# The PV product of an attention kernel in two halves of its columns, with the score products in pairs

## The chip, the cores and the metric

The kernel runs on one core of one Trainium2 chip. Its five engines run side by side and are joined by semaphores: PE (TensorE, the matrix unit), DVE (VectorE), ACT (ScalarE), POOL (GpSimd) and SP (SyncE, which here only starts transfers). PE writes its products to PSUM, eight banks of 128 partitions x 512 fp32. The metric is the device time of one execution in microseconds. Before the change it is 2535.62 us, the median of 3 runs (2533.4 to 2536.08).

## What is computed

The input is x, 4 sequences of 1024 tokens with 128 features. Three layers follow each other: a transformer block with attention and a mixture of experts, a retention layer, and the same transformer block again. Each works on the normalised x and is added to it. The part around the change is the attention of the block, which runs twice:

```python
q = (h @ Wq).reshape(Bb, Ss, H, Dh)      # Bb = 4, Ss = 1024, H = 16 heads, Dh = 8
k = (h @ Wk).reshape(Bb, Ss, H, Dh)
v = (h @ Wv).reshape(Bb, Ss, H, Dh)
scores = jnp.einsum('bqhd,bkhd->bhqk', q, k) / jnp.sqrt(jnp.float32(Dh))
attn = jax.nn.softmax(scores, axis=-1)
ctx = jnp.einsum('bhqk,bkhd->bqhd', attn, v).reshape(Bb, Ss, Dd)
x = x + ctx @ Wo
...
wts, idx = jax.lax.top_k(probs, K)       # K = 2 of 8 experts
h1 = jax.nn.gelu(jnp.einsum('td,edf->etf', xt, W1) + b1[:, None, :])
```

## The kernel before

A layer of attention is 16 groups (`GROUPS`): each is one sequence and four heads. A group has 16 steps s. One step handles 128 keys of one half (512) of the queries for the group's four heads, and at the same time the maxima of the next group:

- `score(layer, g, s, u)`, u = 0 to 3 (L1162): the scores of head u, 128 keys x 512 queries, one product of 51 rows. Its 51 rows are 48 of a product of q and k cut into bf16 parts, and 3 that subtract the row maximum. Heads 0 and 2 lie in the lower 64 rows of the array, heads 1 and 3 in the upper. Each goes to the next bank of a ring of three (`RING`, `s_slot`): PE waits on `s_taken` until ScalarE has read what stood there three slots ago.
- `top(layer, g + 1, s, pair)`, pair = 0, 1 (L1176): the scores of two heads of the next group with the queries on the partitions, a pair of products in the lower and the upper rows, into two banks. `m_slot` waits on `max_taken` until VectorE has read what was put there two slots ago.
- `weigh` (L1189), here called PV: the exponentials of the step two back, times v. Four products, one per head, of 128 rows by 32 columns; each fills its own quarter of the partitions of one bank (`PV_BANK`), and eight steps accumulate there. The fp32 product runs as two passes, so that a trace has eight records for it. v carries a column of ones, which gives the softmax sum.
- `aside` puts single products between S1 and the first maximum pair: the transpose of the maxima ("nm", L1145) at steps 3 and 12, and in groups 0, 1, 4, 5, 8 and 9 the projection of a later chunk of x ("turn" L1103 at step 1, "k" and "q" L1132 at steps 5 and 7, "v" L1138 at step 9). They use a slot of the ring of three.
- `turn_context` (L1103) transposes what PV has summed, at steps 4 and 12, after ScalarE copied it to `ct` (L637, at steps 2 and 10). The next PV of the same bank waits for that copy (`ct_ready`).

On ScalarE, the four exponentials of a step (L657) follow each other, each for a score product; they write `pbuf`, which has room for three steps. On VectorE, each maximum pair is reduced to its maxima by one instruction over 1024 columns (L832); L840 joins the two halves of the keys, L817 and L820 divide the context by the softmax sum. POOL cuts the maxima into bf16 parts (L463 to L466), and SP carries them over DRAM into the rows of q that the scores read (L369, L374).

The order of the instructions of each engine is the order in which the code below issues them. On PE a plain step was S0, S1, T0 (two products), S2, PV (four), S3, T1 (two). Before the first group there is a round of maxima alone (g = -1), and in the last group there are none. After attention come the output projection and the experts (`mix`), which the diff doesn't touch.

Of the kernel before, what the change touches and what calls it, by code (L numbers as in the profile page):

```python
# [38 lines left out]
GROUPS = BATCH * HEADS // GH  # L39
# [28 lines left out]
PV_BANK = 6  # L68
# [10 lines left out]
def asides(g):  # L79

    jobs = {}
    c = chunk_of(g)
    if c is not None:
        jobs.update({1: ("turn", c), 5: ("k", c), 7: ("q", c), 9: ("v", c)})
    if g >= 0:
        jobs[3] = ("nm", g, 1)
    if g + 1 < GROUPS:
        jobs[12] = ("nm", g + 1, 0)
    return jobs


def score_slots():

    order = []
    for layer in range(2):
        order += [(layer, "turn", 0), (layer, "turn", 1)]
        order += [(layer, what, c) for c in range(2) for what in ("k", "q", "v")]
        for g in range(-1, GROUPS):
            jobs = asides(g)
            for s in range(16):  # L100
                if g >= 0:
                    order += [(layer, "s", g, s, 0), (layer, "s", g, s, 1)]
                if s in jobs:
                    order.append((layer,) + jobs[s])
                if g >= 0:
                    order += [(layer, "s", g, s, 2), (layer, "s", g, s, 3)]
    return {key: i for i, key in enumerate(order)}
# [18 lines left out]
S_SLOT = score_slots()  # L126
# [56 lines left out]
def macaron(nc, x_in, small_in, w, out):  # L183
    with ExitStack() as ctx:
# [3 lines left out]
        def sem(name):  # L188
            return ctx.enter_context(nc.semaphore(name))
# [12 lines left out]
        part = {name: small[:, at[name]:at[name] + w] for name, w in SMALL}  # L202
# [22 lines left out]
        with ExitStack() as phase:  # L225
            def at_(name, shape, dt=F32):
                return phase.enter_context(nc.sbuf_tensor(name, shape, dt))

            pbuf = at_("pbuf", [P, 3, GH, 512])
            ks = [at_(f"ks{i}", [P, PAIRS, SEQ], BF16) for i in range(3)]  # L230
            qs = [at_(f"qs{i}", [P, PAIRS, SEQ], BF16) for i in range(3)]
            vst = [at_(f"vst{i}", [P, KT, GH, 32]) for i in range(2)]
# [39 lines left out]
        ps = ctx.enter_context(nc.psum_tensor("ps", [P, 8, 512], F32))  # L272
# [12 lines left out]
        stacks_clear, vst_ready = sem("stacks_clear"), sem("vst_ready")  # L285
        s_filled, s_taken = sem("s_filled"), sem("s_taken")
        max_filled, max_taken = sem("max_filled"), sem("max_taken")
        pv_done, ct_ready = sem("pv_done"), sem("ct_ready")
# [808 lines left out]
        def _(pe):  # L1097
            mm = pe.matmul
# [14 lines left out]
            def m_slot(*key):  # L1113

                i = M_SLOT[key]
                if i >= 2:
                    pe.wait_ge(max_taken, i - 1)
                return m_bank(i)
# [36 lines left out]
            def score(layer, g, s, u):  # L1155

                G = layer * GROUPS + g
                if s % 8 == 0 and u == 0:
                    pe.wait_ge(nm_stacked[s // 8], 32 * (G + 1))
                bank = s_slot(layer, "s", g, s, u)  # L1160
                rows = slice(u % 2 * ROWS, u % 2 * ROWS + SCORE_ROWS)
                mm(ps[:, bank, :], ks[G % 3][rows, u // 2, s % 8 * P:(s % 8 + 1) * P],  # L1162
                   qs[G % 3][rows, u // 2, s // 8 * 512:s // 8 * 512 + 512], start=True,
                   stop=True).then_inc(s_filled, 1)

            def top(layer, g, s, pair):

                G = layer * GROUPS + g
                half, kh, j = s // 8, s % 8 // 4, s % 4
                if s == 0 and pair == 0:  # L1170
                    pe.wait_ge(stack_loaded[G % 3], 16 * LOADS * (G // 3 + 1))
                bank = m_slot(layer, "m", g, s, pair)
                for hb in ((0, 1), (1, 0))[pair]:
                    rows = slice(hb * ROWS, hb * ROWS + MAX_ROW)
                    first = half * 512 + j * P
                    last = mm(ps[:, bank + hb, :], qs[G % 3][rows, pair, first:first + P],  # L1176
                              ks[G % 3][rows, pair, kh * 512:kh * 512 + 512], start=True, stop=True)
                last.then_inc(max_filled, 1)

            def weigh(layer, g, s):  # L1180

                G = layer * GROUPS + g
                pe.wait_ge(s_taken, S_SLOT[layer, "s", g, s, 3] + 1)
                if s == 0:
                    pe.wait_ge(vst_ready, G + 1)
                if s % 8 == 0 and (G or s):
                    pe.wait_ge(ct_ready, G * 2 + s // 8)
                for u in range(GH):
                    last = mm(ps[32 * u:32 * u + 32, PV_BANK, :], vst[G % 2][:, s % 8, u, :],  # L1189
                              pbuf[:, (G * 16 + s) % 3, u, :], start=(s % 8 == 0), stop=(s % 8 == 7))  # L1190
                last.then_inc(pv_done, 1)

            def turn_context(layer, g, half):

                pe.wait_ge(ct_ready, 2 * (layer * GROUPS + g) + half + 1)
                bank = m_slot(layer, "ctx", g, half)
                turn4(bank, ct[:, :]).then_inc(max_filled, 1)

            def attend(layer):
                for g in range(-1, GROUPS):  # L1200
                    jobs = asides(g)
                    for s in range(16):
                        if g >= 0:
                            score(layer, g, s, 0)
                            score(layer, g, s, 1)
                        if s in jobs:
                            aside(layer, jobs[s])
                        if g + 1 < GROUPS:
                            top(layer, g + 1, s, 0)
                        if g >= 0:  # L1210
                            score(layer, g, s, 2)
                        if s < 2 and g >= 1:
                            weigh(layer, g - 1, s + 14)
                        elif s >= 2 and g >= 0:
                            weigh(layer, g, s - 2)
                        if g >= 0:
                            score(layer, g, s, 3)
                        if g + 1 < GROUPS:
                            top(layer, g + 1, s, 1)
                        if s == 4 and g >= 1:  # L1220
                            turn_context(layer, g - 1, 1)
                        if s == 12 and g >= 0:
                            turn_context(layer, g, 0)
                weigh(layer, GROUPS - 1, 14)
                weigh(layer, GROUPS - 1, 15)
                turn_context(layer, GROUPS - 1, 1)

            def chain_parts(layer, c):
# [172 lines left out]
            for layer in range(2):  # L1401
                project(layer)
                attend(layer)
                mix(layer)
                if layer == 0:
                    retain()
# [48 lines left out]
```

## Time and profile before

| | |
|---|---|
| median of 3 runs | 2535.62 us (2533.4 to 2536.08) |
| the profiled execution | 2533.75 us, its span in the trace 2532.0 us |
| busy share of the span | PE 89%, DVE 85%, ACT 66%, PE's weight loads 41%, POOL 33% |
| TensorE clock granted, mean | 0.957 of full speed |
| chain of work that ended last, by engine | PE 55%, DVE 15%, issue 12%, POOL 11%, ACT 6% |
| the same by line, the first three | PE L1189 20%, PE L1162 14%, PE L1176 7% |

The busy share of an engine is a mean over stages with different limits. A product of PE is shown from its start to the end of its pipeline, so that products overlap in the records: how far apart two of them start says more than how long one is. A row of a timeline merges instructions of one kind that follow each other ("x4"); its first number is the start of the first, its second the time to the end of the last. The number behind "idle before" says how long the engine had nothing, and who ended it.

### The profile page before, as it was taken

The page shows a single profiled execution, that of the slowest core. Times are in us where ns is not written, and L with a number is a line of the kernel's source. Part 1 is how long each engine was busy: PE and PEld are TensorE (multiplying, and loading weights), DVE is VectorE, ACT ScalarE, POOL GpSimd, SP SyncE. Part 2 cuts the span into 40 slices and gives each one's busy share as a digit, 9 for nine tenths or more (in the row PEclk, how much of TensorE's full clock was granted, in tenths as well). Part 3 has the DMA queues.
Part 4 walks back from the last instruction along what each step waited for, and adds up shares of the span by engine and source line. Part 5 has one row for each costly group of instructions (what it writes and reads, how often), then busy time and mean ns, then how long its engine had stood idle before and what let it go on. Part 6 is the DMA issues. An engine that isn't in the chain of part 4 may idle for free.

```text
span 2532.0 us, 39142 instructions
## 1 busy us (share of the span) xinstructions
PE 2241.1 (89%) x12680; PEld 1039.6 (41%) x12680; DVE 2155.8 (85%) x2995; ACT 1663.6 (66%) x3025; POOL 825.2 (33%) x877
## 2 busy tenths in 40 slices
PE   2899999999997998899884999999999978999998
PEld 1222222222224776677661222222222226777776
DVE  5889889899964999999657898898899928999999
ACT  1588888788886555555431788788888875555553
POOL 1211221210102666666420201202100005667667
PEclk7799999999998999999895999999999998999999
DMA  2110111101000000010001101100100000111001
GB/s 99 31 48 19 48 31 28 45 25 36 23 2 34 34 34 34 38 63 34 1 9 54 33 22 32 33 27 27 38 17 27 3 2 34 72 39 42 38 38 42
DMA packets 43903, 84.46 MB, mean 33 GB/s; under 512 B 12112, under 2 KB 25680, under 8 KB 41680
## 3 DMA queue, kind: packets, MB, share of 16 engines
q1 hardware_dynamic: 43728, 82.32, 9.8%
q8 instruction: 87, 1.43, 0.2%
q14 instruction: 88, 0.72, 0.1%
HBM read 66.55 MB, written 15.73 MB: 32 GB/s over the span
## 4 chain that ended last, share of the span: by engine, by line
PE 55%; DVE 15%; issue 12%; POOL 11%; ACT 6%; SPq 1%; DMA 1%; POOLq 0%; DVEq 0%; ACTq 0%
PE ps L1189 20%; PE ps L1162 14%; PE ps L1176 7%; POOL hp L528 7%; DVE nmax L832 6%; PE ps L1299 4%; ACT pbuf L657 3%; PE ps L1321 3%; POOL acc L546 3%; DVE hp L998 3%; ACT ct L637 2%; PE ps L1103 2%; PE ps L1132 1%; DVE hp L1002 1%; DVE tmp L968 1%
## 5 line engine op out<-in xcount | busy, mean ns | idle before, releaser
L832 DVE TENSOR_REDUCE nmax<-ps 128x2 f32<-128x1024 f32 x1024 | 1212.4, 1220 | 167.2 <-PE ps L1176 160.2
L657 ACT ACTIVATE pbuf<-ps 128x512 f32<-128x512 f32 x2048 | 1084.0, 601 | 261.9 <-PE ps L1162 255.7
L1162 PE MATMUL ps<-qs,ks 51*128 51x512 bf16 x2048 | 614.9, 386 | 18.2 <-ACT pbuf L657 10.7
L1176 PE MATMUL ps<-ks,qs 48*128 48x512 bf16 x2048 | 523.2, 400 | 83.2 <-DVE nmax L832 48.8
L668 ACT ACTIVATE hr<-ps,small 128x512 f32<-128x512 f32 x512 | 344.1, 688 | 356.9 <-PE ps L1299 167.6
L1189 PE MATMUL ps<-pbuf,vst 128*32 128x512 f32 x4096 | 547.7, 607 | 11.8 <-ACT ct L637 11.8
L528 POOL TENSOR_TENSOR hp<-hr,hp 128x512 fp32r<-128x512 f32 x256 | 429.4, 1678 | 301.1 <-DVE hp L998 301.1
L1321 PE MATMUL ps<-hp,wp 128*128 128x512 f32 x1536 | 448.1, 401 | 24.3 <-DVE tmp L968 17.2
L1299 PE MATMUL ps<-mtp,wp 128*128 128x512 f32 x1536 | 457.5, 407 | 0.0
L998 DVE CAST hp<-hr 128x512 fp32r<-128x512 f32 x512 | 420.6, 843 | 22.3 <-ACT hr L668 15.1
L1162 PEld LDWEIGHTS ps<-qs,ks 51*128 51x128 bf16 x2048 | 154.9, 94 | 663.6 <-ACT pbuf L657 609.3
L463 POOL CAST nm<-negm 128x16 bf16<-128x16 f32 x64 | 13.2, 206 | 1002.4 <-DVE negm L840 1002.4
L1321 PEld LDWEIGHTS ps<-hp,wp 128*128 128x128 f32 x1536 | 290.0, 190 | 106.3 <-DVE tmp L968 20.2
L1299 PEld LDWEIGHTS ps<-mtp,wp 128*128 128x128 f32 x1536 | 288.7, 193 | 64.1
L1176 PEld LDWEIGHTS ps<-ks,qs 48*128 48x128 bf16 x2048 | 116.3, 94 | 231.7 <-DVE nmax L832 151.9
L1002 DVE TENSOR_TENSOR hp<-hr,hp 128x512 fp32r<-128x512 f32 x256 | 179.4, 701 | 0.0
L1189 PEld LDWEIGHTS ps<-pbuf,vst 128*32 128x32 f32 x4096 | 82.7, 108 | 151.3 <-issue 118.4
L546 POOL TENSOR_TENSOR acc<-acc,tmp 128x512 f32<-128x512 f32 x96 | 137.5, 1432 | 1.4 <-DVE tmp L968 1.4
L968 DVE SCALAR_TENSOR_TENSOR tmp<-ps,small,qkv 128x512 f32<-128x512 f32 x128 | 95.0, 742 | 3.2 <-PE ps L1321 3.2
L817 DVE RECIPROCAL rden<-ps 128x16 f32<-128x16 f32 x64 | 15.9, 249 | 79.5 <-PE ps L1103 79.5
L619 ACT ACTIVATE nmt<-ps 48x128 bf16<-48x128 bf16 x64 | 16.9, 265 | 85.6 <-PE ps L1145 85.6
L321 POOL CAST qkv<-qkv 128x512 bf16<-128x512 f32 x24 | 14.7, 614 | 163.2 <-ACT qkv L607 163.2
(141 smaller groups left out, 1280.4 us busy)
## 6 DMA issues: line engine op xcount, KB each, us to landing
qkv<-w_scratch SPq DMA_DIRECT2D x16, 2048.0 KB, 7.1
part_scratch<-qkv SPq DMA_DIRECT2D x32, 384.0 KB, 2.6
ks<-part_scratch SPq DMA_DIRECT2D x384, 32.0 KB
qs<-part_scratch SPq DMA_DIRECT2D x384, 32.0 KB
w_piece<-in_w SPq DMA_DIRECT2D x16, 256.0 KB, 2.7
x<-in_x SPq DMA_DIRECT2D x4, 512.0 KB, 5.1
qs<-nm_scratch SPq DMA_DIRECT2D x128, 6.0 KB
result<-x SPq DMA_DIRECT2D x8, 256.0 KB, 2.0
```

The lines of the kernel that those rows point to most:

```text
L528: pool.tensor_tensor(hp[1][k % 8], hr[k % 4], hp[0][k % 8].bitcast(F32), ALU.subtract).then_inc(hl_odd, 1)
L546: ins = pool.tensor_tensor(acc, acc, tmp[e % 2], ALU.add)
L657: act.activation(pbuf[:, step % 3, u, :], ps[:, s_bank(i), :], ACT.Exp, scale=SCALE).then_inc(s_taken, 1)
L668: act.activation(hr[k % 4], ps[:, k % 4, :], ACT.Gelu_apprx_tanh, bias=b1_sb[:, k // 4, k % 4:k % 4 + 1]).then_inc(gelu_done, 1)
L832: dve.tensor_reduce(nmax[:, half, kh, 4 * j + 2 * u:4 * j + 2 * u + 2], ps[:, bank:bank + 2, :], AX.X, ALU.max, negate=True).then_inc(max_ ...
L998: dve.tensor_copy(hp[0][k % 8], hr[k % 4]).then_inc(hh_ready, 1)
L1002: dve.tensor_tensor(hp[1][(k - 1) % 8], hr[(k - 1) % 4], hp[0][(k - 1) % 8].bitcast(F32), ALU.subtract).then_inc(hl_even, 1)
L1162: mm(ps[:, bank, :], ks[G % 3][rows, u // 2, s % 8 * P:(s % 8 + 1) * P], qs[G % 3][rows, u // 2, s // 8 * 512:s // 8 * 512 + 512], start=True,
L1176: last = mm(ps[:, bank + hb, :], qs[G % 3][rows, pair, first:first + P], ks[G % 3][rows, pair, kh * 512:kh * 512 + 512], start=True, stop= ...
L1189: last = mm(ps[32 * u:32 * u + 32, PV_BANK, :], vst[G % 2][:, s % 8, u, :], pbuf[:, (G * 16 + s) % 3, u, :], start=(s % 8 == 0), stop=(s % ...
L1299: last = mm(ps[:, k % 4, :], w1v[a][:, k // FB, cut], mtp[b][par], start=(i == 0), stop=(i == 2))
L1321: last = mm(ps[:, 4 + e % 2, :], w2v[a][:, e, f, :], hp[b][k % 8], start=(f == 0 and i == 0), stop=(f == FB - 1 and i == 2))
```

## The change

`weigh` gets a `part`: each call makes four products over 256 of the 512 query columns. Part 0 takes the place of the waits; part 1 waits for nothing and signals `pv_done`. The group of eight accumulating steps is opened by the first product of part 0 alone. Part 0 stands behind the first maximum pair, part 1 behind the second; the score products 2 and 3 are issued together between them. The second maximum pair is issued lower rows first, as the first one is.

```diff
--- before.py
+++ after.py
@@ -1170,25 +1170,36 @@
                 if s == 0 and pair == 0:
                     pe.wait_ge(stack_loaded[G % 3], 16 * LOADS * (G // 3 + 1))
                 bank = m_slot(layer, "m", g, s, pair)
-                for hb in ((0, 1), (1, 0))[pair]:
+                for hb in range(2):
                     rows = slice(hb * ROWS, hb * ROWS + MAX_ROW)
                     first = half * 512 + j * P
                     last = mm(ps[:, bank + hb, :], qs[G % 3][rows, pair, first:first + P],
                               ks[G % 3][rows, pair, kh * 512:kh * 512 + 512], start=True, stop=True)
                 last.then_inc(max_filled, 1)
 
-            def weigh(layer, g, s):
+            def weigh(layer, g, s, part):
 
                 G = layer * GROUPS + g
-                pe.wait_ge(s_taken, S_SLOT[layer, "s", g, s, 3] + 1)
-                if s == 0:
-                    pe.wait_ge(vst_ready, G + 1)
-                if s % 8 == 0 and (G or s):
-                    pe.wait_ge(ct_ready, G * 2 + s // 8)
+                if part == 0:
+                    pe.wait_ge(s_taken, S_SLOT[layer, "s", g, s, 3] + 1)
+                    if s == 0:
+                        pe.wait_ge(vst_ready, G + 1)
+                    if s % 8 == 0 and (G or s):
+                        pe.wait_ge(ct_ready, G * 2 + s // 8)
+                cut = slice(256 * part, 256 * part + 256)
                 for u in range(GH):
-                    last = mm(ps[32 * u:32 * u + 32, PV_BANK, :], vst[G % 2][:, s % 8, u, :],
-                              pbuf[:, (G * 16 + s) % 3, u, :], start=(s % 8 == 0), stop=(s % 8 == 7))
-                last.then_inc(pv_done, 1)
+                    last = mm(ps[32 * u:32 * u + 32, PV_BANK, cut], vst[G % 2][:, s % 8, u, :],
+                              pbuf[:, (G * 16 + s) % 3, u, cut], start=(s % 8 == 0 and part == 0),
+                              stop=(s % 8 == 7), skip_group_check=True)
+                if part == 1:
+                    last.then_inc(pv_done, 1)
+
+            def weigh_late(layer, g, s, part):
+
+                if s < 2 and g >= 1:
+                    weigh(layer, g - 1, s + 14, part)
+                elif s >= 2 and g >= 0:
+                    weigh(layer, g, s - 2, part)
 
             def turn_context(layer, g, half):
 
@@ -1207,22 +1218,20 @@
                             aside(layer, jobs[s])
                         if g + 1 < GROUPS:
                             top(layer, g + 1, s, 0)
+                        weigh_late(layer, g, s, 0)
                         if g >= 0:
                             score(layer, g, s, 2)
-                        if s < 2 and g >= 1:
-                            weigh(layer, g - 1, s + 14)
-                        elif s >= 2 and g >= 0:
-                            weigh(layer, g, s - 2)
-                        if g >= 0:
                             score(layer, g, s, 3)
                         if g + 1 < GROUPS:
                             top(layer, g + 1, s, 1)
+                        weigh_late(layer, g, s, 1)
                         if s == 4 and g >= 1:
                             turn_context(layer, g - 1, 1)
                         if s == 12 and g >= 0:
                             turn_context(layer, g, 0)
-                weigh(layer, GROUPS - 1, 14)
-                weigh(layer, GROUPS - 1, 15)
+                for s in (14, 15):
+                    for part in range(2):
+                        weigh(layer, GROUPS - 1, s, part)
                 turn_context(layer, GROUPS - 1, 1)
 
             def chain_parts(layer, c):
```

PE in a plain step (step 7 of group 13) of the first layer, before (qs,ks: a score product, L1162; ks,qs: a maximum product, L1176; pbuf,vst: PV, L1189):

```order
L1162 MATMUL ps<-qs,ks 128x512 [waits s_taken] x2
L1176 MATMUL ps<-ks,qs 128x512 [waits max_taken]
L1176 MATMUL ps<-ks,qs 128x512
L1162 MATMUL ps<-qs,ks 128x512 [waits s_taken]
L1189 MATMUL ps<-pbuf,vst 32x512 [waits s_taken]
L1189 MATMUL ps<-pbuf,vst 32x512 x3
L1162 MATMUL ps<-qs,ks 128x512 [waits s_taken]
L1176 MATMUL ps<-ks,qs 128x512 [waits max_taken]
L1176 MATMUL ps<-ks,qs 128x512
```

The same step after (L1191 is PV there):

```order
L1162 MATMUL ps<-qs,ks 128x512 [waits s_taken] x2
L1176 MATMUL ps<-ks,qs 128x512 [waits max_taken]
L1176 MATMUL ps<-ks,qs 128x512
L1191 MATMUL ps<-pbuf,vst 32x256 [waits s_taken]
L1191 MATMUL ps<-pbuf,vst 32x256 x3
L1162 MATMUL ps<-qs,ks 128x512 [waits s_taken] x2
L1176 MATMUL ps<-ks,qs 128x512 [waits max_taken]
L1176 MATMUL ps<-ks,qs 128x512
L1191 MATMUL ps<-pbuf,vst 32x256 x4
```

S3 has moved ahead of PV and beside S2; the four PV products of 512 columns have become two sets of four of 256 (L1191), with the wait on the first set only, and each set stands behind a maximum pair.

PE in the last group of the first layer, where there are no maxima, steps 9 and 10, before (the four score products in a row are S3 of one step and S0 to S2 of the next):

```order
L1162 MATMUL ps<-qs,ks 128x512 [waits s_taken] x4
L1189 MATMUL ps<-pbuf,vst 32x512 [waits s_taken]
L1189 MATMUL ps<-pbuf,vst 32x512 x3
L1162 MATMUL ps<-qs,ks 128x512 [waits s_taken] x4
L1189 MATMUL ps<-pbuf,vst 32x512 [waits ct_ready,s_taken]
L1189 MATMUL ps<-pbuf,vst 32x512 x3
L1162 MATMUL ps<-qs,ks 128x512 [waits s_taken] x4
```

The same place after:

```order
L1162 MATMUL ps<-qs,ks 128x512 [waits s_taken] x2
L1191 MATMUL ps<-pbuf,vst 32x256 [waits s_taken]
L1191 MATMUL ps<-pbuf,vst 32x256 x3
L1162 MATMUL ps<-qs,ks 128x512 [waits s_taken] x2
L1191 MATMUL ps<-pbuf,vst 32x256 x4
L1162 MATMUL ps<-qs,ks 128x512 [waits s_taken] x2
L1191 MATMUL ps<-pbuf,vst 32x256 [waits ct_ready,s_taken]
L1191 MATMUL ps<-pbuf,vst 32x256 x3
L1162 MATMUL ps<-qs,ks 128x512 [waits s_taken] x2
L1191 MATMUL ps<-pbuf,vst 32x256 x4
```

The score products come in twos, each followed by half of a PV. The wait for the context copy (`ct_ready`) stands on the first half.

On DVE, ACT and SP the order of the instructions is the same before and after, and on POOL too.

## Rows read from the trace of the kernel before

**Rows 1.** Page: line, engine, op, out<-in | busy, mean ns | idle before, releaser

```profile
L832 DVE TENSOR_REDUCE nmax<-ps 128x2 f32<-128x1024 f32 x1024 | 1212.4, 1220 | 167.2 <-PE ps L1176 160.2
```

**Rows 2.** Windows: PE, PEld, DVE, ACT, POOL busy (records), clock, DMA share, GB/s

```profile
83.00:779.00 696.00, 653.55 (x4283) 166.81 (x4281) 586.66 (x575) 568.12 (x1111) 110.67 (x237) 0.99 0.10 30
```

**Rows 3.** Waits: who waited for whom, us in total, times, longest

```profile
PEld ps L1162 <- ACT pbuf L657: 609.3, 1016, 1.0
```

**Rows 4.** Timeline, plain steps: start, us, engine, line, op [idle before]

```profile
544.96 1.06 PE L1189 MATMUL ps<-pbuf,vst 128*32 128x512 f32 x8
...
545.41 0.61 PE L1189 MATMUL ps<-pbuf,vst 128*32 128x512 f32 x4
...
545.95 0.39 PE L1162 MATMUL ps<-qs,ks 51*128 51x512 bf16 x1
...
546.38 2.06 ACT L657 ACTIVATE pbuf<-ps 128x512 f32<-128x512 f32 x4 [0.33 <-PE ps L1162]
...
546.63 0.39 PE L1176 MATMUL ps<-ks,qs 48*128 48x512 bf16 x2
...
547.03 0.39 PE L1162 MATMUL ps<-qs,ks 51*128 51x512 bf16 x1
547.34 0.16 PEld L1189 LDWEIGHTS ps<-pbuf,vst 128*32 128x32 f32 x8 [0.23 <-issue]
547.35 1.06 PE L1189 MATMUL ps<-pbuf,vst 128*32 128x512 f32 x8
```

**Rows 5.** Timeline: context at step 4, and two maxima back to back

```profile
540.86 0.63 PE L1103 MATMUL ps<-small,ct 128*128 128x128 f32 x4 [0.16 <-DVE nmax L832]
...
541.42 0.39 PE L1162 MATMUL ps<-qs,ks 51*128 51x512 bf16 x2
...
541.89 0.25 DVE L817 RECIPROCAL rden<-ps 128x16 f32<-128x16 f32 x1
...
542.46 1.23 DVE L832 TENSOR_REDUCE nmax<-ps 128x2 f32<-128x1024 f32 x1
...
551.38 2.36 DVE L832 TENSOR_REDUCE nmax<-ps 128x2 f32<-128x1024 f32 x2
```

**Rows 6.** Timeline, step 2: the context copy and the PV behind it

```profile
533.10 0.59 ACT L637 ACTIVATE ct<-ps 128x512 f32<-128x512 f32 x1
...
533.83 1.06 PE L1189 MATMUL ps<-pbuf,vst 128*32 128x512 f32 x8 [0.19 <-ACT ct L637]
```

**Rows 7.** Timeline, step 3: last exponential of step 2, transpose, maximum pair

```profile
535.25 1.57 ACT L657 ACTIVATE pbuf<-ps 128x512 f32<-128x512 f32 x3
...
536.00 0.22 PE L1145 MATMUL ps<-ident_b,nm 128*128 128x128 bf16 x1 [0.34 <-ACT pbuf L657]
...
536.14 0.39 PE L1176 MATMUL ps<-ks,qs 48*128 48x512 bf16 x2
```

**Rows 8.** Timeline, step 7 of a chunk group: the q projection

```profile
1626.42 1.10 PE L1132 MATMUL ps<-ah,small 128*128 128x512 f32 x2 [0.34 <-ACT pbuf L657]
1627.45 0.39 PE L1176 MATMUL ps<-ks,qs 48*128 48x512 bf16 x2
```

**Rows 9.** Timeline of POOL: the first cast after each group's start

```profile
1608.22 0.20 POOL L463 CAST nm<-negm 128x16 bf16<-128x16 f32 x1 [19.45 <-DVE negm L840]
...
1654.39 0.21 POOL L463 CAST nm<-negm 128x16 bf16<-128x16 f32 x1 [21.18 <-DVE negm L840]
...
1696.27 0.20 POOL L463 CAST nm<-negm 128x16 bf16<-128x16 f32 x1 [19.87 <-DVE negm L840]
```

**Rows 10.** Timeline of ACT, last group: its first and last context copy

```profile
742.51 0.59 ACT L637 ACTIVATE ct<-ps 128x512 f32<-128x512 f32 x1
...
778.47 0.60 ACT L637 ACTIVATE ct<-ps 128x512 f32<-128x512 f32 x1 [1.29 <-PE ps L1189]
```

**Rows 11.** Timeline and window: two PVs with nothing between, first layer's end

```profile
776.48 1.92 PE L1189 MATMUL ps<-pbuf,vst 128*32 128x512 f32 x16
...
776.47:777.81 1.34, 1.34 (x17) 0.41 (x16) 0.00 (x0) 0.60 (x1) 0.00 (x0) 1.00 0.00 0
```

## Prediction

> **What bounds the kernel now.** I read the page's groups by line first. The costliest is VectorE's maximum (L832, 1212 us, idle 167 us before it) [rows 1], which lies in attention alone. The table by stage says how attention stands: its first stage lasts 696 us of 2532, with PE busy 654, DVE 587, ACT 568 us, and the clock at its upper level, 2.4 GHz (0.99) [rows 2]; there is a second like it. The change touches these two stages only, and both PE and DVE look nearly full there. The list of waits then shows what the shares hide: PE's loads for the score products (L1162) waited 609 us for ScalarE's exponentials, 1016 times [rows 3].
>
> The timeline of one plain step tells why [rows 4]. I call the four score products S0 to S3, their exponentials e0 to e3, the two pairs of maximum products T0 and T1. A loop closes over PE and ACT: S3 starts at 545.95, e3 at 546.38 (0.43), S2 of the next step needs e3's bank (ring of three) and starts at 547.03 (0.65), PV follows at 547.35 (0.32), and S3 comes only behind it, 0.99 later (544.96 to 545.95). 0.43 + 0.65 + 0.32 + 0.99 = 2.39 us, and plain steps repeat at that. VectorE isn't the bound in it: two maxima back to back are 1.14 apart (a pair spans 2.36, one lasts 1.22) [rows 5], 2.28 a step. PE isn't either: T0 ends its stream about 546.84 (546.63 and a spacing of 0.21 to 0.23) and S2 starts at 547.03, so 0.19 is wait.
>
> **The change part by part.**
>
> *S3 moves ahead of PV.* e3 no longer waits for PV's 0.99, and the 2.39 loop is gone. Two new ones take its place. S3 needs e0's bank: S0, +0.43, +0.65 = 1.08. S1 of the next step needs e2's: S2, +1.08. Both are inside half a step as long as that is over 1.08.
>
> *S2 and S3 stand side by side.* They use different halves of the rows. Before, a step had five slots: S3, T1, S0 and S1 shared three of 0.23 each (0.68 from 545.95 to T0 at 546.63), then came T0, and S2 alone. Now there are four (S0 with S1, T0, S2 with S3, T1), each both halves wide. One slot of 0.21 goes.
>
> *PV as two halves.* One PV is four head products of two passes, eight records that span 1.06; two PVs with nothing between them (sixteen records) span 1.92 [rows 4, 11], so a pass streams 0.86 / 2 = 0.43. First pass to second is 0.45 (544.96 to 545.41), second pass to S3 0.54, so 0.11 for the change of kind out. S2 to PV is 0.32 against 0.21 streamed, so 0.10 for the change in. A half has 0.235 + 0.215 + 0.11 = 0.56 to 0.57, plus 0.32 from the slot before. The added price is one more change in and out: 0.21 a step. The weights are loaded again in each half, so there are eight more loads a step. All eight of a PV are done in 0.16 from its start (547.34) [rows 4]: those of the second pass are in before a first pass of 0.235 has ended, and those of the first cost the 0.02 by which 0.45 exceeds 0.43, which I count in each half. No row shows a 256-column half. From below: no change of kind at all between, 0.21 less a step; from above: a half costs as much as a whole, 0.99, which is +0.84 a step. I take the halved streams, since the stream is what the passes scale by in rows 4 and 11.
>
> A page speaks against this edit: the Trainium skill, TensorEngine Tiling (Array Packing), Key Properties, says that changing the tiling mode drains the engine. The rows agree in kind (0.10 in, 0.11 out), at less than the whole tail of a product (0.39 long, next one 0.23 later). If every change cost that tail of about 0.16, a step would be some 0.22 longer than I sum, a group of 16 steps 3.5 us, and the gain below would be gone; by the rows it is 0.10 to 0.11 each, and that is in the sum.
>
> *PE's sum for a plain step:* 2 x (0.23 + 0.32 + 0.565) = 2.23 us. DVE's is 2.28. So in plain steps both are late together, about 0.15 under 2.39. The margin of the two ring loops is 1.115 - 1.08 = 0.03 us.
>
> *What interrupts the steps, per group of 16.* PE falls behind here, and VectorE (which may lag by about half a microsecond before PE must wait for it) takes up the difference.
> - Twice the context copy. PV starts 0.73 after it (533.10 to 533.83) [rows 6]. With S2 at 0: e2 0.43, e3 0.92 (exponentials follow each other by 0.49: four span 2.06, three 1.57 [rows 4, 7]), the copy 1.41, PV possible at 2.14; PE would be there at 0.23 + 0.32 + 0.565 + 0.23 + 0.32 = 1.67. +0.47 each.
> - Twice the transpose of the maxima. It starts 0.75 after e3 (535.25 to 536.00), the maximum product 0.14 later [rows 7]: 0.92 + 0.75 + 0.14 = 1.81 against 1.35. +0.46 each.
> - Twice the context's transposes, 540.86 to 541.42: +0.56 each, and about 0.1 once for a bank of VectorE's. On DVE the context costs 541.89 to 542.46, 0.57 [rows 5].
>
> PE: 16 x 2.23 = 35.7, + 0.94 + 0.92 + 1.12 + 0.1 = 38.8. DVE: 32 x 1.14 = 36.5, + 2 x 0.57 = 37.6. PE ends last: 38.8. Before, such a group is 1696.27 - 1654.39 = 41.88 [rows 9]. Gain 3.1 each, and there are 9 of them per layer, 18.
>
> *Groups that also project a chunk* (6 per layer, 12): 1654.39 - 1608.22 = 46.17 before [rows 9]. k, q and v hold PE 1.03 (1626.42 to 1627.45) [rows 8], again from 0.75 after e3: 0.92 + 0.75 + 1.03 = 2.70 against 1.35, +1.35, twice; k stands behind the context's transposes where e3 is long done, about +1.1; the turn is four transposes (0.56, as above), +0.88. Together 4.7, so 43.5. Gain 2.7 each. VectorE has slack there.
>
> *The last group* of a layer has no maxima; its steps are 2.39 too (35.96 us from the copy at 742.51 to the last, over 14 steps and the tail) [rows 10]. After, the longest loop is S0, e0, S3 (1.08), PV (0.32), back to S0 (0.57): 1.97 a step. 16 x 0.42 = 6.7, less about 1.9, since the copy, the maxima and the transposes no longer lie in slack. Gain 4.8, twice. The group ahead of the first (maxima only) and all else on DVE, ACT, POOL and SP keeps its order and price. The maxima's round trip over DRAM has several microseconds in hand before step 8 and before the next group.
>
> Sum: 18 x 3.1 + 12 x 2.7 + 2 x 4.8 = 55.8 + 32.4 + 9.6 = 98 us off the profiled execution's 2533.75: 2436. The median of the runs is 1.9 higher: **2437 us**.
>
> **The rivals.**
> - *VectorE alone bounds the groups* (chance 0.10). For it: it needs only 37.6 in a plain group, and switches between halves may overlap more than I count. Against: the copies and transposes lie on PE. 18 x 4.2 + 12 x 3.5 + 2 x 6 = 130 us less: 2406.
> - *The ring takes the wait back* (0.17). The margins are 0.03 us; if e0 or e2 comes 0.05 to 0.1 late for S3 or S1, as a queue of four exponentials can make it, each step grows by 0.1 to 0.15: 480 x 0.1 to 0.15 = 48 to 72 us of the gain gone, 2485 to 2509. Against: ACT needs only four times 0.49, 1.96 of 2.23.
> - *Slower: PE is fed too slowly* (0.10). A step now carries 16 weight loads and 16 products; after, 24 and 24, in 2.23 us: 46 ns each. Above 50 ns (2.39 / 48) the step is longer than before. Densest in the trace are 33 in 1.34 us, 41 ns [rows 11], and that is short enough to have been queued; the long run in attention is 75 ns (32 in 2.39). At 55 ns: 2.64 a step, +0.25 x 496 steps = +124 us and no gain elsewhere: about 2660. At 50 to 51, equal to before. The same place would show if a half's second pass waited for its weights. The Trainium skill, TensorE: Matmul & The Clock Gate, Back-to-back issue gap, gives about 62 ns per product where products aren't decoded in hardware; counted for products only, 24 x 62 ns = 1.5 us, it would stay hidden, and counted for loads too it would make 3.0. In rows 4 eight weight loads of PV come within 0.16; no row shows the rate over a long run.
> - *The change of kind is dearer beside a short half* (0.05). At 0.15 more a step the gain is about used up: 2525 to 2545.
>
> **How the numbers follow.** Forecast 0.58 (its own range 2418 to 2455, from 0.04 a step either way); VectorE 0.10; ring 0.17; feeding 0.10; dearer change 0.05. Differences under 0.2% (5 us) are what a measurement of this kernel can't tell from none. Faster: 0.58 + 0.10 + 0.17 + 0.02 = 0.87; same 0.03; slower 0.10. The range from 2406 to 2490 holds the forecast, VectorE's case and the near part of the ring's.
>
> **What would show it.** S3 beginning beside S2 and e3 directly behind e2. A PV half taking 0.56 to 0.57 from its first product to the next score product; over 0.65 the forecast falls. Steps of 2.23 to 2.28; casts of the maxima (L463) 38.8 apart in plain groups. PE's loads for L1162 waiting for ACT far less than 609 us, those for L1176 waiting for DVE somewhat more. Last group's steps at 1.97. If L1162 still waits for L657 every step, it is the ring; if PE idles with "issue" before PV's loads, it is feeding.

## The result, and the profile after

| | before | after |
|---|---|---|
| median | 2535.35 us (4 runs, the 3 shown before and one more, 2533.4 to 2536.08) | 2440.06 us (4 runs, 2435.55 to 2442.39) |
| ratio, 95% interval | | 0.9623 [0.9607, 0.9640] |
| profiled execution, its span | 2533.75, 2532.0 us | 2435.55, 2433.7 us |

The forecast was 2437 us. The page after, with the group that answers to [rows 1] first, then the exponentials and PV (columns as there):

```profile
L832 DVE TENSOR_REDUCE nmax<-ps 128x2 f32<-128x1024 f32 x1024 | 1184.5, 1218 | 100.2 <-PE ps L1176 97.5
L657 ACT ACTIVATE pbuf<-ps 128x512 f32<-128x512 f32 x2048 | 1107.7, 597 | 133.3 <-PE ps L1162 114.3
L1191 PE MATMUL ps<-pbuf,vst 128*32 128x256 f32 x8192 | 655.3, 392 | 27.5 <-ACT ct L637 27.5
```

VectorE does the same 1024 reductions and waits 67 us less for them. PV has 8192 records of 256 columns. The first attention stage by windows, against the row of [rows 2]:

```profile
83.00:735.00 652.00, 628.21 (x6349) 179.92 (x6345) 577.20 (x582) 586.75 (x1113) 111.61 (x239) 0.99 0.11 32
```

The granted clock is the same, and PE is busy 628 of 652 us. The 44 us by which this window is shorter are not the whole gain, since it reaches 5 us past the end of attention: the last context copy starts at 778.47 in [rows 10] and at 729.38 after (below), 49.1 us earlier. Two such stages make the 98.2 us by which the profiled execution is shorter. The timeline of PE in plain steps after, which answers to [rows 4]:

```profile
556.86 0.64 PE L1191 MATMUL ps<-pbuf,vst 128*32 128x256 f32 x8
...
557.43 0.10 PEld L1162 LDWEIGHTS ps<-qs,ks 51*128 51x128 bf16 x2 [0.41 <-issue]
557.43 0.39 PE L1162 MATMUL ps<-qs,ks 51*128 51x512 bf16 x2
...
557.66 0.38 PE L1176 MATMUL ps<-ks,qs 48*128 48x512 bf16 x2
...
557.97 0.64 PE L1191 MATMUL ps<-pbuf,vst 128*32 128x256 f32 x8
558.54 0.10 PEld L1162 LDWEIGHTS ps<-qs,ks 51*128 51x128 bf16 x2 [0.41 <-ACT pbuf L657]
558.54 0.39 PE L1162 MATMUL ps<-qs,ks 51*128 51x512 bf16 x2
```

Three distances are to be seen: 0.57 from a half of PV to the score pair, 0.23 from that to the maximum pair, 0.31 to the next half. That is 1.11 a half-step and 2.22 a step, with no wait of PE's products in it. The rows of the loads (PEld) show how a label misleads: the same 0.41 before the score loads is put down to nothing ("issue") at 557.43 and to ScalarE at 558.54, and both times the score pair starts 0.57 behind PV. It is the time in which the loads have nothing to do because PV streams. That is why the list of waits still has a large entry where [rows 3] had 609.3:

```profile
PEld ps L1162 <- ACT pbuf L657: 358.2, 901, 0.8
```

The lengths of the groups by POOL's casts, as in [rows 9]:

```profile
1543.57 0.20 POOL L463 CAST nm<-negm 128x16 bf16<-128x16 f32 x1 [17.42 <-DVE negm L840]
...
1586.93 0.20 POOL L463 CAST nm<-negm 128x16 bf16<-128x16 f32 x1 [19.14 <-DVE negm L840]
...
1625.66 0.20 POOL L463 CAST nm<-negm 128x16 bf16<-128x16 f32 x1 [18.27 <-DVE negm L840]
```

A group with a chunk takes 43.36 us (before 46.17), a plain one 38.73 (41.88). The last group, first to last context copy, took 35.96 in [rows 10]; after, 32.09:

```profile
697.29 0.61 ACT L637 ACTIVATE ct<-ps 128x512 f32<-128x512 f32 x1
...
729.38 0.60 ACT L637 ACTIVATE ct<-ps 128x512 f32<-128x512 f32 x1 [1.33 <-PE ps L1191]
```

What is left between the plain steps shows in steps 2 and 3 of a plain group after, the stretch of [rows 6, 7]:

```profile
542.71 0.38 PE L1176 MATMUL ps<-ks,qs 48*128 48x512 bf16 x2
542.76 0.61 ACT L637 ACTIVATE ct<-ps 128x512 f32<-128x512 f32 x1
...
543.52 0.64 PE L1191 MATMUL ps<-pbuf,vst 128*32 128x256 f32 x8 [0.43 <-ACT ct L637]
...
545.20 0.39 PE L1162 MATMUL ps<-qs,ks 51*128 51x512 bf16 x2
545.74 0.22 PE L1145 MATMUL ps<-ident_b,nm 128*128 128x128 bf16 x1 [0.15 <-ACT pbuf L657]
545.89 0.39 PE L1176 MATMUL ps<-ks,qs 48*128 48x512 bf16 x2
```

PV could start 0.31 behind the maximum pair, at 543.02, and starts at 543.52: 0.50 for the context copy. The maximum pair comes 0.69 behind the score pair instead of 0.23: 0.46 for the transpose of the maxima.

### The profile page after: what moved, and what is told of

It is laid out like the page before. It is cut to its first block, busy times and chain, and to the rows that moved or that the text cites. A ratio compares the mean times of both kernels' runs of the same rounds, so it can differ in the third digit from the quotient of the medians.

```text
span 2433.7 us, 47334 instructions
## 1 busy us (share of the span) xinstructions
PE 2188.1 (90%) x16776; PEld 1066.5 (44%) x16776; DVE 2132.4 (88%) x2995; ACT 1696.2 (70%) x3025; POOL 824.3 (34%) x877
## 4 chain that ended last, share of the span: by engine, by line
PE 57%; DVE 12%; POOL 10%; issue 10%; ACT 9%; SPq 1%; DMA 1%; POOLq 0%; DVEq 0%; ACTq 0%
PE ps L1191 20%; PE ps L1162 12%; PE ps L1176 7%; ACT pbuf L657 7%; POOL hp L528 6%; PE ps L1308 5%; PE ps L1330 4%; DVE nmax L832 3%; PE ps L1103 3%; POOL acc L546 3%; DVE hp L998 3%; ACT ct L637 2%; PE ps L1132 1%; DVE hp L1002 1%; DVE tmp L968 1%
## 5 line engine op out<-in xcount | busy, mean ns | idle before, releaser
L832 DVE TENSOR_REDUCE nmax<-ps 128x2 f32<-128x1024 f32 x1024 | 1184.5, 1218 | 100.2 <-PE ps L1176 97.5
L657 ACT ACTIVATE pbuf<-ps 128x512 f32<-128x512 f32 x2048 | 1107.7, 597 | 133.3 <-PE ps L1162 114.3
L1191 PE MATMUL ps<-pbuf,vst 128*32 128x256 f32 x8192 | 655.3, 392 | 27.5 <-ACT ct L637 27.5
L1176 PE MATMUL ps<-ks,qs 48*128 48x512 bf16 x2048 | 409.8, 397 | 67.0 <-DMA qs<-part_scratch 34.8
L1162 PE MATMUL ps<-qs,ks 51*128 51x512 bf16 x2048 | 410.8, 390 | 0.0
L1191 PEld LDWEIGHTS ps<-pbuf,vst 128*32 128x32 f32 x8192 | 164.5, 108 | 420.4 <-issue 237.8
L1162 PEld LDWEIGHTS ps<-qs,ks 51*128 51x128 bf16 x2048 | 104.0, 93 | 409.6 <-ACT pbuf L657 358.2
L1176 PEld LDWEIGHTS ps<-ks,qs 48*128 48x128 bf16 x2048 | 102.5, 96 | 136.3 <-DVE nmax L832 84.0
```

The costliest lines, as they stand in the source:

```text
L657: act.activation(pbuf[:, step % 3, u, :], ps[:, s_bank(i), :], ACT.Exp, scale=SCALE).then_inc(s_taken, 1)
L832: dve.tensor_reduce(nmax[:, half, kh, 4 * j + 2 * u:4 * j + 2 * u + 2], ps[:, bank:bank + 2, :], AX.X, ALU.max, negate=True).then_inc(max_ ...
L1191: last = mm(ps[32 * u:32 * u + 32, PV_BANK, cut], vst[G % 2][:, s % 8, u, :], pbuf[:, (G * 16 + s) % 3, u, cut], start=(s % 8 == 0 and par ...
```

## Experiments

All times are medians, with the ratio to the kernel before in the same set of runs. "A step" is the distance between the first exponentials of two plain steps in the trace.

| | us | ratio, 95% interval | step, us |
|---|---|---|---|
| changed kernel again (e8) | 2435.30 | 0.9606 [0.9593, 0.9619] | 2.22 |
| e1 pair, PV whole | 2576.80 | 1.0185 [1.0147, 1.0223] | 2.61 |
| e2 halves together, old order | 2535.76 | 1.0008 [0.9998, 1.0018] | 2.40 |
| e3 PV in three places | 2549.44 | 1.0058 [1.0041, 1.0075] | 2.46 |
| e4 cut at 192 | 2446.64 | 0.9653 [0.9637, 0.9669] | 2.29 |
| e5 quarters | 2438.50 | 0.9619 [0.9603, 0.9635] | 2.23 |
| e6 old order in the maximum pair | 2436.51 | 0.9608 [0.9592, 0.9624] | 2.22 |
| e7 cut at 320 | 2475.00 | 0.9762 [0.9746, 0.9778] | 2.29 |
| e9 asides late | 2430.52 | 0.9584 [0.9571, 0.9597] | 2.22 |
| e10 and maximum pairs early | 2438.67 | 0.9619 [0.9605, 0.9632] | 2.22 |
| e11 and doubled maxima | 2444.07 | 0.9640 [0.9627, 0.9654] | 2.22 |

**e1: the score products paired, PV not halved.**

The diffs of e1 to e9 are against the changed kernel; `...` marks what is left out. Here part 0 returns without a product and part 1 has the waits.

```diff
-                cut = slice(256 * part, 256 * part + 256)
+                cut = slice(0, 512)
+                if part == 0:
+                    return
...
-                        weigh_late(layer, g, s, 0)
                         if g >= 0:
                             score(layer, g, s, 2)
                             score(layer, g, s, 3)
+                        weigh_late(layer, g, s, 1)
                         if g + 1 < GROUPS:
                             top(layer, g + 1, s, 1)
-                        weigh_late(layer, g, s, 1)
```

> The score products 2 and 3 together as in the change, but PV whole, once, behind them and ahead of the second maximum pair. My theory (loops of waits): S3 needs e0's bank, 1.08 us behind S0, and all of PV comes behind it: 1.08 + 0.32 + 0.99 + 0.23 = 2.62 us a plain step (2.39 before, 2.23 after the change), so about 2640 us, slower than before. Rival (what helped is that S3 stands beside S2 and e3 no longer waits for PV; the halves only cost a change of kind): PE needs 2.00 us a step, VectorE's 2.28 would decide, 2440 us or less.

The step is 2.61 us as the loop of waits gave it, and the rival with 2.28 falls. The timeline of a step in e1 (its PV is L1193):

```profile
651.16 0.38 PE L1162 MATMUL ps<-qs,ks 51*128 51x512 bf16 x2
...
651.60 0.38 PE L1162 MATMUL ps<-qs,ks 51*128 51x512 bf16 x1
...
652.23 0.39 PE L1162 MATMUL ps<-qs,ks 51*128 51x512 bf16 x1 [0.25 <-ACT pbuf L657]
...
652.54 1.07 PE L1193 MATMUL ps<-pbuf,vst 128*32 128x512 f32 x8
```

S0 is at 651.16 and S2 at 651.60; S3 has to wait until 652.23, 1.07 behind S0, for e0's bank, and all of PV comes after it. So the pairing alone makes the kernel slower. The total was 63 us below what I expected, because the interruptions cost less beside this longer loop: a chunk group takes 46.18 us there, 4.4 over its 16 steps of 2.61, where the changed kernel has 7.8 over its steps, and a plain one 44.08, 2.3 over them, where the changed kernel has 3.2. That the idle time of PE in the loop takes them up is the likely reason.

**e2: the halving alone.**

```diff
-                for hb in range(2):
+                for hb in ((0, 1), (1, 0))[pair]:
...
-                        weigh_late(layer, g, s, 0)
                         if g >= 0:
                             score(layer, g, s, 2)
+                        weigh_late(layer, g, s, 0)
+                        weigh_late(layer, g, s, 1)
+                        if g >= 0:
                             score(layer, g, s, 3)
...
-                        weigh_late(layer, g, s, 1)
```

> The order of the kernel before (S2, PV, S3), PV as two sets of 256 columns right behind each other. It prices the halving by itself. My theory: 0.02 us per set for its first weight load, 2.41 us a plain step, 2540 to 2547 us. Rival (halved sets are slow to feed or to load): 0.1 us or more a step, over 2585 us.

0.01 us a step at most, and the time is that of the kernel before (interval 0.9998 to 1.0018). Halving by itself costs next to nothing and brings nothing. My 0.02 per set was at least twice too high.

**e3: one more change of kind.**

```diff
-                cut = slice(256 * part, 256 * part + 256)
+                cut = (slice(0, 256), slice(256, 384), slice(384, 512))[part]
...
+                        weigh_late(layer, g, s, 1)
                         if g + 1 < GROUPS:
                             top(layer, g + 1, s, 1)
-                        weigh_late(layer, g, s, 1)
+                        weigh_late(layer, g, s, 2)
```

> As the changed kernel, but the second half of PV in two sets of 128 columns, one ahead of the second maximum pair and one behind it. One change of kind in and out more per step. My theory: 0.10 in, 0.11 out and 0.02 for the set, 2.46 us a plain step, about 2550 us. If a change cost the whole tail of a product (0.16 each way): 2.57 a step, about 2610 us. If changes cost nothing beside the waits: 2440 us.

2.46 us a step and 2549 us, both as summed. The timeline of PE in e3:

```profile
641.53 0.39 PE L1162 MATMUL ps<-qs,ks 51*128 51x512 bf16 x2
641.85 0.42 PE L1191 MATMUL ps<-pbuf,vst 128*32 128x128 f32 x8
642.20 0.39 PE L1176 MATMUL ps<-ks,qs 48*128 48x512 bf16 x2
642.52 0.43 PE L1191 MATMUL ps<-pbuf,vst 128*32 128x128 f32 x8
642.88 0.39 PE L1162 MATMUL ps<-qs,ks 51*128 51x512 bf16 x2
```

A set of 128 columns streams for 2 x 0.107 = 0.21 (a quarter of the 0.43 of [rows 4, 11] per pass), and the next kind starts 0.35 to 0.36 after it. The price of a change in and out is 2.46 - 2.22 = 0.24 us a step, a little over the 0.21 read in [rows 4], and short of the 0.32 that a full tail of 0.16 each way would make. So two places gain and three don't: e3 is 15 us slower than the kernel before.

**e4 and e7: where the cut lies.**

```diff
-                cut = slice(256 * part, 256 * part + 256)
+                cut = (slice(0, 192), slice(192, 512))[part]    # e4
+                cut = (slice(0, 320), slice(320, 512))[part]    # e7
```

> As the changed kernel with PV cut at column 192 instead of 256: the same work, but the first half-step is 0.11 us shorter, the second longer. My theory: the ring of three banks has a margin of 0.03 us at the even cut; S3 now has to wait for e0's bank until 1.08 us behind S0, so a plain step is 1.08 + 1.22 = 2.30 us and the whole about 2470 us. Rival (PE's work alone decides): no change, 2440 us.

> The mirror of the cut at 192: PV cut at column 320, so the first half-step is 0.11 us longer and the second shorter. The cut at 192 gave plain steps of 2.29 us. My theory: now the other ring wait binds, S1 of the next step on e2's bank, 1.08 us behind S2: again 1.22 + 1.08 = 2.30 us a plain step, and about 2447 us as there. Rival (only the first half matters, or what the cut at 192 showed was something else): 2.22 us a step, 2440 us.

Both give a step of 2.29 us with the same work, so both ring waits exist where the loops of the prediction put them. Timeline of e4, where the second score pair follows the shorter part:

```profile
600.07 0.39 PE L1162 MATMUL ps<-qs,ks 51*128 51x512 bf16 x2
...
601.06 0.17 PEld L1162 LDWEIGHTS ps<-qs,ks 51*128 51x128 bf16 x2 [0.30 <-issue]
601.07 0.46 PE L1162 MATMUL ps<-qs,ks 51*128 51x512 bf16 x2
```

At 600.07 the two products start together (0.39 in all). At 601.07 the second is 0.07 later (0.46 in all): S3 waits for e0's bank until 1.07 behind S0. Timeline of PE in e7, where it is the pair behind the second, shorter part:

```profile
613.50 0.39 PE L1162 MATMUL ps<-qs,ks 51*128 51x512 bf16 x2
...
614.51 0.46 PE L1162 MATMUL ps<-qs,ks 51*128 51x512 bf16 x2
```

The same 0.07, for S1 this time. So at the even cut the margin is 0.03 to 0.04 and it holds. The totals weren't what I wrote. e7 lost 40 us to the changed kernel (e8) instead of about 11, and that is what its steps make: a plain group is 39.98 long, 1.25 more than 38.73, where 16 x 0.07 is 1.12, and a chunk group 44.69, 1.3 more. I had taken over e4's total, and e4 is the exception: it lost 11 us instead of 30, with a plain group of 39.29, only 0.56 more, and a chunk group of 43.36, as long as in the changed kernel. The traces show where the two part: the two steps around a context copy take 4.84 us together in e4, 4.94 in the changed kernel and 5.11 in e7, and the step with the v projection 3.64, 3.88 and 4.10. Behind such a stall the first part of PV stands between PE and the next score pair, so that a short first part is worth something there. That reason fits, but no run tests it.

**e5: feeding and loading PE.**

```diff
-                cut = slice(256 * part, 256 * part + 256)
+                for lo, hi in (((0, 128), (128, 256)), ((256, 384), (384, 512)))[part]:
+                  cut = slice(lo, hi)
```

> As the changed kernel, but each half of PV is two sets of 128 columns right behind each other: 40 weight loads and 40 products per step instead of 24 and 24, with the same streams and the same changes of kind. It asks whether PE can be fed and loaded at that rate. My theory: one or two hundredths of a microsecond per extra set, 2.24 to 2.28 us a plain step (28 ns per load or product), 2440 to 2460 us. Rival (feeding or weight loads are near their limit, so the halves too are just fast enough): at the densest 41 ns seen so far 3.3 us a step, over 2900 us; if only the second pass's load (0.11 us and its issue) is exposed behind a pass of 0.107: some 0.2 us a step, 2540 us.

40 loads and 40 products fit in a step of 2.23 us, 28 ns each, 0.01 over the changed kernel. The timeline of PE in e5:

```profile
601.90 0.64 PE L1192 MATMUL ps<-pbuf,vst 128*32 128x128 f32 x16
602.48 0.39 PE L1162 MATMUL ps<-qs,ks 51*128 51x512 bf16 x2
```

The same place in the timeline of its weight loads:

```profile
601.90 0.38 PEld L1192 LDWEIGHTS ps<-pbuf,vst 128*32 128x32 f32 x16 [0.43 <-issue]
```

Sixteen loads take 0.38 and the whole 0.58 from PV's start to the next score product, where eight took 0.57. The rival by which this change could have been slower is refuted with a wide margin: it needs 46 ns an instruction, and 28 are sustained here.

**e6: the order inside the second maximum pair.**

```diff
-                for hb in range(2):
+                for hb in ((0, 1), (1, 0))[pair]:
```

> As the changed kernel, with the second maximum pair's products in the old order, upper rows first: this one part undone. My theory: both rows' queues hold one product of each slot either way, no change, 2436 to 2443 us. Rival (the order of the two decides whether the pair runs beside the pair before it): 0.2 us a step, 2540 us.

No change: 2436.5 us, against 2435.3 for the changed kernel (e8) and 2440.1 on record. That part of the diff does nothing for the time.

**e8: the changed kernel again, and the spread.**

> The changed kernel unchanged, as the base for the other kernels of this set. Its four runs so far gave 2435.6 to 2442.4 us where the kernel before stayed within 3 us. My theory for the spread: the first group after a stage with an idle PE starts with the TensorE clock at its lower level and how many of its steps (4.3 us instead of 2.2) fall into that varies. I expect 2436 to 2443 us with steps of 2.22, 38.73 us a plain group, 43.37 us a group with a chunk.

2433.15 to 2438.99 us over five runs. Its profiled execution was the slowest of them, 3.4 us over the profiled one of the result. Windows of the first group in the profile of the result:

```profile
88.00:92.00 4.00, 4.00 (x24) 0.84 (x24) 3.37 (x4) 2.67 (x6) 0.00 (x0) 0.50 0.15 57
92.00:96.00 4.00, 4.00 (x41) 1.07 (x37) 3.43 (x4) 3.06 (x7) 0.00 (x0) 0.94 0.02 3
```

And the same windows in e8:

```profile
88.00:92.00 4.00, 4.00 (x22) 0.79 (x18) 3.48 (x3) 2.61 (x6) 0.00 (x0) 0.50 0.23 68
92.00:96.00 4.00, 4.00 (x26) 0.85 (x25) 2.45 (x2) 2.26 (x5) 0.00 (x0) 0.50 0.00 0
```

The column behind POOL's is the granted clock: 0.50, the lower level of 1.2 GHz, with PE busy throughout. From 92 to 96 it is back at 0.94 in the one and still at 0.50 in the other. That group is 2.6 us longer there, and the first group of the second layer 1.6: 4.2 in all for a difference of 3.4 to 3.5. For these two executions the difference is thus accounted for; that the other runs spread for the same reason is only likely.

**e9: the asides behind PV's first half.**

```diff
-                        if s in jobs:
-                            aside(layer, jobs[s])
                         if g + 1 < GROUPS:
                             top(layer, g + 1, s, 0)
                         weigh_late(layer, g, s, 0)
+                        if s in jobs:
+                            aside(layer, jobs[s])
```

> As the changed kernel, with the asides (transposes and projections that use a slot of the ring) behind the first half of PV instead of ahead of the first maximum pair. My theory of the interruptions: such a product waits for e3's bank until 0.75 us behind e3's start, and PE stands still for about 0.3 us; behind PV's first half the bank is free when PE gets there. Gain 0.3 us for each of the four projections of a chunk group, 12 x 1.2 = 14 us; nothing for the transposes of the maxima, where S3 would wait for e1's bank as long anyway: 2425 us. Rival (the stall is made up elsewhere, by VectorE's lag or the ring): no change.

A third of it came at most: 2430.5 us, 4.8 under e8 with intervals that just overlap. Plain groups are 38.63 long (38.73), chunk groups 43.20 (43.37), which makes 18 x 0.10 + 10 x 0.17 = 3.5 us without the first group of each layer. The length of those two differs from one execution to the next with the clock, as e8 shows, so the rest may be chance. Only the q projection's step gained about the 0.3 us expected (0.28, 3.57 to 3.29), and the next step gave back 0.11. Why the rest didn't come shows at a transpose of the maxima in e9's timeline of PE:

```profile
606.23 0.23 PE L1145 MATMUL ps<-ident_b,nm 128*128 128x128 bf16 x1
606.39 0.68 PE L1162 MATMUL ps<-qs,ks 51*128 51x512 bf16 x2
```

The transpose no longer waits, but the score pair behind it is 0.68 long instead of 0.39: S3 waits 0.29 for a bank. A slot more in a ring of three is paid for either way. It has the lowest median of the versions that I ran.

**e10: both maximum pairs ahead of the PV that waits for the context copy.** The diff is against e9.

```diff
+                        if s in (2, 10) and g + 1 < GROUPS:
+                            top(layer, g + 1, s, 1)
                         weigh_late(layer, g, s, 0)
...
-                        if g + 1 < GROUPS:
+                        if s not in (2, 10) and g + 1 < GROUPS:
                             top(layer, g + 1, s, 1)
```

> As the kernel with late asides, and in steps 2 and 10 both maximum pairs stand ahead of PV's first half, which waits there for the context copy. My theory: PV can't start before 0.73 us behind the copy's start; the second maximum pair can go into that stall as soon as VectorE has freed its banks, and about 0.13 us of 0.47 is won each time, 62 times, 8 us: 2418 us. Rival (VectorE frees the banks no earlier than PV could start): no gain, 2425 us, or a few us lost.

It is 8 us slower than e9. The rival held in the plain groups, 39.24 us against 38.63. The timeline of e10:

```profile
581.52 0.60 ACT L637 ACTIVATE ct<-ps 128x512 f32<-128x512 f32 x1
...
582.34 0.39 PE L1176 MATMUL ps<-ks,qs 48*128 48x512 bf16 x2 [0.50 <-DVE nmax L832]
582.65 0.64 PE L1191 MATMUL ps<-pbuf,vst 128*32 128x256 f32 x8
```

VectorE frees the banks at 582.34. PV could have started 0.76 behind the copy, at 582.28, so the pair that was to fill the stall delayed PV by 0.37. Some of that comes back at once, since the pair is out of the way of PV's second half, but a step with such a copy is 0.25 longer in the end, and step 11 another 0.10. In the chunk groups, where VectorE has slack, the theory held: the same steps are 0.14 shorter there (2.24 against 2.38) and the group takes 43.03 against 43.20. So the early pair pays where VectorE isn't behind, and the 18 plain groups outweigh the 12 others.

**e11: the maximum products of group 0 made twice.** The diff is against e10. The extra products write the values that are there already.

```diff
-                for hb in range(2):
+                for hb in (0, 1) * (2 if g == 0 else 1):
```

> As the kernel before it in this set, with each maximum product of group 0 made twice into the same bank (the same values; only added work). In the round of maxima alone PE is 53% busy at the lower clock and VectorE decides. My theory: a nearly full PE gets the upper clock during that round, group 0 no longer starts at the lower one, and takes 43.4 us less the gains above in both layers instead of 44.4 and 46.3: 4 us won, and less spread. Rival (the clock in group 0 has to do with something else, or the doubled products delay VectorE): no gain or up to 10 us lost.

The rival again: 5.4 us slower than e10. Windows of e11 in the round of maxima:

```profile
60.00:70.00 10.00, 8.85 (x36) 1.05 (x32) 9.98 (x10) 0.00 (x0) 0.66 (x4) 0.50 0.01 2
```

PE is 88% busy for the whole window and the granted clock stays at 0.50, while VectorE gets its banks later: seventeen reductions span 20.11 us, 19.32 in e10. Group 0 isn't shorter for it: 44.8 and 44.5 us in the two layers, 44.6 and 44.8 in e10. So this much more work on PE didn't raise the clock earlier; what would isn't shown.

## Why the prediction was right

*What bounds the kernel before.* The loop S3, e3, S2, PV of 2.39 us is shown by both halves of the change taken apart. e2 leaves the order and changes only PV's cut: the step stays. e1 puts S3 ahead of PV but leaves PV whole: the loop named in the prediction takes over with 1.07 from S0 to S3 and all of PV behind it. Only the two together open the ring, since then just half a PV stands between a score product and the next that needs its bank.

*PV in halves.* 0.56 to 0.57 was the forecast and 0.57 is in the trace. The change of kind cost 0.24 in e3 against 0.21 summed, where a full tail each way would be 0.32. The loads of the second pass are hidden even behind passes of half that length (e5).

*PE's sum.* 2.23 us forecast, 2.22 measured. *The interruptions:* 0.47 and 0.46 forecast for copy and transpose, 0.50 and 0.46 found; a plain group 38.8 against 38.73, a chunk group 43.5 against 43.36. *The last group:* steps of 1.97 forecast, 1.96 found; 4.8 gained forecast; 3.87 between its copies, which leaves out its first two steps, at 0.43 each some 4.7 with them. The sum by measured terms is 18 x 3.15 + 12 x 2.81 + 2 x 4.7 = 99.8 us for 98.2 measured; the first group of each layer, with its steps at the lower clock, gained 2.3 instead of 2.81.

*The number itself* owes something to luck. The profiled execution was to take 2436 us and took 2435.55, but it was the fastest of four that reach to 2442.39, and by the medians the gain is 95 us on record and 100 in e8's set. So the sum is confirmed to a few us, and not to half of one.

*VectorE* was to lag and take up the stalls: in the plain steps after it reduces back to back (three span 3.48 us), and it waits 67 us less in all. It isn't the bound, but it is closer to it than the sum said: it is busy 37.9 us of a plain group's 38.73, not 37.6, and e10 shows that PE has to wait for it as soon as a maximum pair comes early.

*What I had wrong.* "L1162 waiting for ACT far less": 358 us of 609 are left in the list, though the waits are gone from the products; I took the label of the loads for a wait. I also expected the loads for L1176 to wait somewhat more for VectorE: they wait less, 84.0 us in the list after against 151.9 before. The rival *the ring takes the wait back* had its condition right and its chance too high: the margin of 0.03 us is real, and e4 and e7 show what it costs to use it up, 0.07 a step for 64 columns. The feeding rival was further off than its 0.10: 28 ns against the 50 from which it would decide. And my expectations of totals in e1, e4, e7, e9 and e10 failed where the plain steps were right: I counted the interruptions as fixed prices, and what one costs depends on the order and the loop around it.

## What to carry to other kernels

In a queue worked in order, look for a long instruction between the filling of a buffer and the next filling that needs it back, and compute the loop: fill, read, free, refill. If the long one can be cut, put the pieces at equal distances, no shorter than one round of the ring (here 1.11 us against 1.07); more pieces only pay changes of kind, and moving the fill without cutting the long one can make the loop longer. When one loop goes, list what each interruption waits for under the new order before adding up, since prices read beside idle time don't hold without it.

## What the runs showed of the hardware

- Products in the lower and the upper half of the rows don't keep a common order. In a step before the change, the maximum pair behind S3 is issued upper rows first:

```profile
545.96 0.60 PE L1176 MATMUL ps<-ks,qs 48*128 48x512 bf16 x2
546.19 0.38 PE L1162 MATMUL ps<-qs,ks 51*128 51x512 bf16 x1
```

  The record at 545.96, beside S3, is the one that signals `max_filled`, the second of the pair and in the lower rows; the first, in the rows of S3, starts at 546.18 beside S0. So S3, the pair, S0 and S1 take three slots of 0.23 us, and in e6 the order inside a pair makes no difference.
- Between two other kinds, a PV set of 512, 256 and 128 columns takes 0.99, 0.57 and 0.35 us: a part that goes with the columns (0.86, 0.43, 0.21) and some 0.14 that doesn't. Sets of 128 columns right behind each other pay that once (e5), and 40 loads and 40 products fit in 2.23 us.
- The granted clock stayed at the lower level, 0.50, through a round in which PE was 87 to 89% busy (e11), and in other executions through stretches in which PE was busy throughout, from 88 to 96 us in e8, where it was back at 0.94 from 92 to 96 in the profile of the result. How long it stays differs from one execution to another.
